# Two combine-and-route stages reordered: sums two batches ahead, logits before ranks, small weights loaded one stage sooner

## The chip, the cores and the metric

The kernel runs on one core of a Trainium2 chip. The metric is the time of one execution on the device in microseconds (us). Three runs of the kernel before gave 2446.49, 2455.0 and 2457.12 us, a median of 2455.0. The profiled execution was a fourth one.

## The reference

Four layers on 4 batches of 512 tokens of 256 float32 numbers (T = 2048 tokens), each layer `x = x + ffn(cond(x))`. What the change touches is the way from one mixture of experts to the next work:

```python
x = x + L0_ffn(L0_cond(x))         # causal attention, ternary linear layer
x = x + L1_ffn(L1_cond(x))         # attention with relative bias; mixture f1: top 2 of 8, capacity, gelu
x = x + L2_ffn(L2_cond(x, cond))   # mixture c2 plus shared expert; mixture f2: top 1 of 8, capacity, relu
x = x + L3_ffn(L3_cond(x))         # attention with relative bias; mixture f3: top 2 of 8, swiglu

# L2_cond
logits = (x @ wt.T + repeat(g @ wg.T, s, axis=0)) / 2
topk_w, topk_idx = top_k(softmax(logits), 2);  topk_w = topk_w / (topk_w.sum(-1) + 1e-20)
y = sum over the two experts of topk_w * ((leaky(x @ w_gate[e]) * (x @ w_up[e])) @ w_down[e])
p = (leaky(x @ sw_gate) * (x @ sw_up)) @ sw_down          # shared expert, every token
y = y + p
# L2_ffn: eidx = argmax(softmax(x @ Wr)); each expert takes its first T/8 tokens (rank = running count)
# L3_cond, bias: h = silu(ln(pos @ w0 + b0, g0)); h = silu(ln(h @ w1 + b1, g1)); h @ w2 + b2
```

## The kernel before

The program is a row of stages. Within a stage every engine has its own instruction list, written out by hand in the order in which it runs, and engines wait for each other on semaphores; between stages all engines meet. Three stages are touched besides two that load weights.

**Stage A** comes after the experts of f1. SP loads the experts' rows (`Combine.sync`, L2027: 8 transfers of 512 KB). DVE adds them to the tokens, batch by batch, with 8 `scalar_tensor_tensor` a batch (`Combine.vector`, L2037: "the sum"). Then tokens are routed to c2. For each batch: PE turns the 4 token tiles (`tensor_turn`, L1491, 8 transposes), ACT copies the turned tokens (L1457), PE makes the logits (`tensor`, L1504 and, for the conditioned router, L1507), DVE takes the best two experts (`vector_ahead`, L1545 to L1570), PE counts ranks (`tensor_after`, L1516 to L1521), DVE makes row numbers (`vector`, L1580 to L1587), and POOL scatters the rows with one indirect DMA for each token tile and choice (`pool`, L1442). After the last batch `vector_last` (L1594 to L1629) makes the list of expert tiles. The same stage runs the shared expert as 18 pipelined steps (16 token tiles): on PE L2082, L2090 and L2098, on ACT L2107 and further, on DVE L2124 and L2129. The weights of the router are loaded by the stage itself, behind the rows:

```python
def sync(self, sp):            # Router, L1401
    sp.dma_start(self.wr_rows[:], self.w_router)...      # 3 loads where the router is conditioned, 1 where not
for b in range(B):             # combine_and_route, PE: turn, logits, two shared steps, ranks, then the next batch
    part.tensor_turn(pe, b)
    part.tensor(pe, b)
    ...
    part.tensor_after(pe, b)
```

The **tile stage** follows: the experts of c2, 40 tiles of tokens, whose rows SP loads one by one (L1865), with four loads of 1 MB of f2's weights between (L1870, `ahead`).

**Stage B** has the same function as stage A, `combine_and_route`, with c2's rows, f2's router and no shared expert, but the relative bias of layer 3 (`RelativeBias`, `rel`): its 8 weights are loaded behind the router's, and its DVE, ACT, POOL and PE steps stand between the batches. `first_hidden` (L230 to L234), `statistics`, `root` on POOL, `normalise` (L254) and `scale` (L260) come after batch 0, the second half after batch 2, `last_product` at the end.

**Stage C** is the input stage of layer 3's attention (`attention_inputs`): DVE first sums f2's rows for all 4 batches (L2037, in `beside`), then takes statistics and normalises, and at last makes the null key and the mask (L435 to L453), for which the product with `inw_wkv` on PE (L651) waits.

Everywhere a copy of the tokens for the second choice (`copy_rows`) is kept for two batches, and the bank of the logits is free again when the ranks of that batch are read (`rank_read`).

Of the kernel before, what the change touches and what calls it, by code (L numbers as in the profile page):

```python
# [20 lines left out]
P = 128  # L21
# [157 lines left out]

class RelativeBias:  # L180
# [5 lines left out]
    def __init__(self, nc, c, l, w, rev, stack, banks):  # L186
        m = Memory(nc, stack, f"rel{l}", side="right")
        self.nc, self.c, self.l, self.w, self.rev = nc, c, l, w, rev
        self.w0, self.b0, self.g0, self.b1, self.g1 = (m.sb(n, [P, D]) for n in ("w0", "b0", "g0", "b1", "g1"))
        self.w1, self.w2, self.b2 = m.sb("w1", [P, KD, D]), m.sb("w2", [P, KD, H]), m.sb("b2", [H, 1])  # L190
# [8 lines left out]
        names = "loaded dist_made hidden link mv_ready rooting rstd_ready scaled pre_ready act_ready t_ready t_copied h_ready o_ready row_ready".split()  # L199
        (self.loaded, self.dist_made, self.hidden, self.link_s, self.mv_ready, self.rooting, self.rstd_ready, self.scaled, self.pre_ready, self.act_ready,  # L200
# [151 lines left out]
def attention_inputs(nc, c, l, iw, stack, block, relative=None):  # L352
# [16 lines left out]
    rel = relative(stack, qt_ps[:].rearrange("p h s -> p (h s)").rearrange("p (k s) -> p k s", k=KD)) if relative is not None else None  # L369
# [8 lines left out]
    if rel is not None:  # L378
        @block.sync
        def _(sp):  # L380
            rel.load(sp)
            rel.store(sp)
# [6 lines left out]
    def _(pool):  # L389
        pool.memset(c.kmask[:], 0.0).then_inc(cleared, 1)  # L390
        for b in range(B):
            pool.wait_ge(mv_ready, QT * (b + 1))
            inverse_root(pool, c, mv[:, b, :, 1], ALU.add, EPS, rooting, b + 1, rstd_ready)
        if cosine:
            pool.wait_ge(null_summed, 1)
            inverse_root(pool, c, nn[:], ALU.max, 1e-24, null_floored, 1, null_root)
# [26 lines left out]
    def _(dve):  # L423
# [928 lines left out]

class Router:
# [1078 lines left out]
```

## Time and profile before

| | |
|---|---|
| median of 3 runs | 2455.0 us |
| the profiled execution, its own time | 2444.63 us |
| its span in the profile | 2442.8 us |
| mean granted TensorE clock | 0.919 of 2.4 GHz |
| PE busy | 2081.4 us (85%) |
| DVE, ACT, POOL busy | 1110.2 (45%), 995.5 (41%), 588.9 us (24%) |
| stage A, from SP's first load to the next stage's | 1202.3 to 1325.3 us |
| tile stage | 1325.3 to 1446.3 us |
| stage B | 1446.3 to 1537.5 us |
| stage C | from 1665.1 us |

Times of rows are microseconds from the span's start. PE is the matmul side of TensorE, SPq the time in which SP's queue writes transfers. A bracket at the end of a row tells how long the engine was idle before it and whose work ended that. A granted clock of 1.00 is 2.4 GHz and one of 0.50 is 1.2 GHz; between them it is the mean of a stretch that had both.

### The profile page before, as it was taken

The numbers are of one execution on the slowest core, as the hardware profiler recorded it, in microseconds if no ns is written. First come the engines' busy times: TensorE is split into PE (matmuls) and PEld (weight loads), VectorE is DVE, ScalarE is ACT, GpSimd is POOL, SyncE is SP. The second block draws the span as 40 slices with busy tenths as digits, with TensorE's granted clock in tenths as the row PEclk, the third lists the DMA queues.
The fourth block names the chain that finished last, engine by engine and source line by source line (L and its number), as shares of the span: only waits on it lengthen the run. The fifth ranks groups of instructions, "written<-read, shape, count | busy, mean of one in ns | idle before, by whom it ended". The sixth has DMA issues, their size and how long they took to land. (4 is left out here: it accounts for less than half of the span.)

```text
span 2442.8 us, 47321 instructions
## 1 busy us (share of the span) xinstructions
PE 2081.4 (85%) x16296; PEld 1466.3 (60%) x16297; DVE 1110.2 (45%) x3373; ACT 995.5 (41%) x2622; POOL 588.9 (24%) x970
## 2 busy tenths in 40 slices
PE   6899999797999994999677854895979999959994
PEld 3477767555777673666455643683557776736663
DVE  5488871455888632010043325115568884321112
ACT  2378871165788611111112321121658774212221
POOL 2121210284111124111131322113831111321111
PEclk9999999898999996999868975897989999969997
DMA  2374402003433113322213240551010003131113
GB/s 79 85 231 133 146 24 90 0 1 104 125 106 106 55 37 103 103 98 90 78 44 110 92 133 26 192 173 40 1 45 21 20 11 129 46 119 44 45 43 111
DMA packets 157136, 197.94 MB, mean 81 GB/s; under 512 B 15315, under 2 KB 130222, under 8 KB 156940
## 3 DMA queue, kind: packets, MB, share of 16 engines
q1 hardware_dynamic: 145228, 169.09, 22.4%
q0 software_dynamic: 11712, 26.26, 3.0%
q8 instruction: 119, 1.95, 0.3%
q14 instruction: 77, 0.63, 0.1%
HBM read 120.60 MB, written 88.90 MB: 86 GB/s over the span
## 5 line engine op out<-in xcount | busy, mean ns | idle before, releaser
L907 ACT ACTIVATE att_pr<-all_h,att_nmax 128x128 f32<-128x128 f32 (+3 forms) x768 | 422.1, 552 | 92.2 <-DVE att_nmax L863 91.0
L965 PEld LDWEIGHTS att_t_ps<-all_ident,att_pr 64*128 64x128 f32 x3840 | 183.6, 139 | 108.2 <-issue 42.9
L965 PE MATMUL att_t_ps<-all_ident,att_pr 64*128 64x64 f32 x3840 | 188.4, 223 | 11.0 <-DVE att_pt L871 10.1
L843 POOL COPY att_rexp<-att_rinv 128x512 f32<-128x512 f32 x96 | 58.6, 610 | 514.8 <-DVE att_rinv L875 514.8
L1133 PE MATMUL out_y_ps<-outw_wo,mem_qt 128*128 128x256 f32 x768 | 178.0, 385 | 0.0
L871 DVE COPY att_pt<-att_t_ps 128x256 f32<-128x256 f32 (+3 forms) x240 | 177.5, 739 | 1.0 <-PE att_t_ps L965 1.0
L1739 PE MATMUL exp_f_h_ps<-exp_f_xs_t,cw_f_w 128*128 128x512 f32 (+1 forms) x512 | 172.2, 495 | 1.5 <-DVE exp_f_xs_t L1776 1.5
L1751 PE MATMUL exp_f_y_ps<-cw_f_w,exp_f_hid 128*128 128x256 f32 x768 | 168.4, 379 | 0.0
L1133 PEld LDWEIGHTS out_y_ps<-outw_wo,mem_qt 128*128 128x128 f32 x768 | 143.5, 191 | 25.0 <-issue 6.8
L1751 PEld LDWEIGHTS exp_f_y_ps<-cw_f_w,exp_f_hid 128*128 128x128 f32 x768 | 144.8, 190 | 19.5 <-issue 0.5
L1806 ACT ACTIVATE exp_f_hid<-exp_f_h_ps 128x512 f32<-128x512 f32 (+1 forms) x128 | 62.4, 490 | 223.3 <-PE exp_f_h_ps L1739 223.1
L863 DVE CUSTOM_DVE_ANT_0 all_h<-att_s_ps,att_bias,mem3k_nsn 128x128 f32<-128x128 f32 (+3 forms) x256 | 130.2, 546 | 46.1 <-PE att_s_ps L953 33.1
L863 DVE CUSTOM_DVE_ANT_0 all_h<-att_s_ps,att_bias,mem1k_nsn 128x128 f32<-128x128 f32 (+3 forms) x256 | 130.2, 546 | 45.9 <-PE att_s_ps L953 33.9
L863 DVE CUSTOM_DVE_ANT_0 all_h<-att_s_ps,att_bias,mem0k_nsn 128x128 f32<-128x128 f32 (+3 forms) x256 | 130.2, 547 | 42.8 <-POOL att_bias L826 24.8
L907 ACT ACTIVATION_READ_ACCUMULATOR att_pr<-all_h,att_nmax 128x1 f32 x768 | 144.9, 189 | 0.0
L1739 PEld LDWEIGHTS exp_f_h_ps<-exp_f_xs_t,cw_f_w 128*128 128x128 f32 x512 | 99.4, 195 | 68.6 <-issue 61.0
L919 ACT ACTIVATE att_pt<-att_t_ps 128x1024 f32<-128x1024 f32 (+1 forms) x144 | 116.7, 810 | 31.5 <-PE att_t_ps L965 31.5
L669 PE MATMUL in_q_ps<-inw_wq,all_xt 128*128 128x512 f32 x256 | 120.3, 615 | 2.8 <-ACT all_xt L566 2.8
L1718 POOL DMA_INDIRECT expert_f<-exp_f_ys,exp_f_idx x48 | 46.7, 972 | 305.6 <-DVE exp_f_ys L1785 254.5
L1982 DVE COPY til_f_xs_t<-til_f_x_ps 128x256 f32<-128x256 f32 x40 | 17.0, 425 | 195.6 <-PE til_f_x_ps L1904 195.6
L988 PE MATMUL att_o_ps<-att_pt,mem0k_v 128*64 128x128 f32 x1280 | 97.7, 282 | 1.5 <-DVE mem_qt L882 0.4
L988 PE MATMUL att_o_ps<-att_pt,mem1k_v 128*64 128x128 f32 x1280 | 97.7, 282 | 1.5 <-DVE mem_qt L882 0.4
(395 smaller groups left out, 3900.5 us busy)
## 6 DMA issues: line engine op xcount, KB each, us to landing
sorted_c<-all_zero SPq DMA_DIRECT2D x8, 2056.0 KB, 13.8
sorted_f<-all_zero SPq DMA_DIRECT2D x8, 2056.0 KB, 11.9
cw_f_w<-in_L_ffn_w_dram SPq DMA_DIRECT2D x16, 1024.0 KB, 8.0
cw_f_w<-in_L_ffn_W_dram SPq DMA_DIRECT2D x16, 1024.0 KB, 8.0
com_f_rows<-expert_f SPq DMA_DIRECT2D x20, 512.0 KB, 6.7
band<-rev SPq DMA_DIRECT2D x2, 4096.0 KB, 19.4
att_bias<-band SPq DMA_DIRECT2D x32, 256.0 KB, 3.2
til_c_xs<-sorted_c SPq DMA_DIRECT2D x40, 128.5 KB, 2.1
```

Source lines behind the costliest of these rows:

```text
L669: last = nc.tensor.matmul(q_ps[t % 2][:, n, :], c.xt[:, k, P * t:P * (t + 1)], wq[:, k, S * n:S * (n + 1)], start=(k == 0), stop=(k == KD ...
L843: pool.tensor_copy(rexp[:], group_ap(rinv, G).unsqueeze(3).to_broadcast([P, B, 2, DH])).then_inc(rexp_ready, 1)
L863: nc.vector.tensor_tensor_reduce(sc[p % 4][:, hh, 0:n], s_ps[(2 * p + hh) % 3][:, 0:n], bias_ap(i, q, hh), -1.0, c.nsn[:, b, q, h:h + 1], ...
L871: nc.vector.tensor_copy(*pt_and_turned(p)).then_inc(t_copied[e % 2], 1)
L907: nc.scalar.activation(pr[p % 4][:, hh, 0:n], sc[p % 4][:, hh, 0:n], ACT.Exp, scale=-1.0, bias=nmax[:, b, q, h:h + 1], accum_out=rsum[:, b ...
L919: nc.scalar.activation(*pt_and_turned(p), ACT.Copy).then_inc(t_copied[e % 2], 1)
L965: last = nc.tensor.transpose(t_ps[e % 2][:, n, (q + 1) * hh + kb, :], pr[p % 4][d, hh, P * kb:P * (kb + 1)], c.ident[d, d])
L988: last = nc.tensor.matmul(o_ps[DH * hh:DH * (hh + 1), p % B, :], c.v[:, QT * b + kb, :], pt[p % 4][:, P * ((q + 1) * hh + kb):P * ((q + 1) ...
L1133: nc.tensor.matmul(y_ps[b % 2][:, q, :], c.out_t[:, p, S * b + P * q:S * b + P * (q + 1)], wo[:, p, :], start=(p == 0), stop=False)
L1739: last = nc.tensor.matmul(h_ps[f % 4][:, 0:cap], w1_sb[n][:, k, P * f:P * (f + 1)], xs_t[n][:, k, :], start=(k == 0), stop=(k == KD - 1))
L1751: last = nc.tensor.matmul(y_ps[(YT * n + t // 2) % 2][:, t % 2, :], hid[n][:, f, P * t:P * (t + 1)], w2_sb[n][:, f, :], start=(f == 0), st ...
L1806: nc.scalar.activation(hid[n][:, f, :], h_ps[f % 4][:, 0:cap], func).then_inc(hid_ready, 1)
```

## The change

The small weights move into the stage before (`RouterWeights`, `RelativeWeights`): three loads for stage A go ahead of the other `ahead` loads of f1's experts, nine loads for stage B go ahead of the four 1 MB loads of the tile stage. `combine_and_route` is replaced by one function for each stage. Both sum two batches ahead; the logits of batch b+1 stand before the ranks of batch b, which a semaphore of its own (`logits_read`) allows; the copies for the second choice are kept for all 4 batches; in stage A `vector_last` stands after shared step 10 instead of last; in stage B the bias's first half stands ahead of the sums. The condition's part of the logits is one matmul for a batch, ahead of the others, where it was one for each token tile. Stage C makes the null key and mask first and takes sums, statistics and normalisation in turn.

```diff
-        for t in range(QT):
-            for k in range(KD):
-                last = self.nc.tensor.matmul(self.l_ps[:, t, :], self.xt_of(b)[:, k, P * t:P * (t + 1)], self.wr[:, k, :], start=(k == 0),
-                                             stop=(k == KD - 1 and self.cond is None))
-            if self.cond is not None:
-                last = self.nc.tensor.matmul(self.l_ps[:, t, :], self.g_t[:, b:b + 1].to_broadcast([DH, P]), self.wg_t[:], start=False, stop=True)
+            pe.wait_ge(self.logits_read, b)
+            if self.one_bank:
+                pe.wait_ge(self.rank_read, b)
+        if rw.conditioned:
+            self.nc.tensor.matmul(self.l_ps[:, 0:QT, :], rw.g_t[:, b:b + 1].to_broadcast([DH, P]), rw.wg_t[:].unsqueeze(1).to_broadcast([DH, QT, E]),
+                                  start=True, stop=False)
...
-            copy_rows = m.sb("copy_rows", [P, 2 * QT, W])[:] if mx.top == 2 else None
+            copy_rows = m.sb("copy_rows", [P, NT, W])[:] if mx.top == 2 else None
...
+def combine_and_share(nc, c, com, part, shx, block):   # stage A, DVE:
+        com.vector(dve, 0)
+        com.vector(dve, 1)
+        part.vector_ahead(dve, 0)
+        com.vector(dve, 2)
+        shx.vector(dve, 0)
+        part.vector(dve, 0)
+        part.vector_ahead(dve, 1)
+        shx.vector(dve, 1)
+        com.vector(dve, 3)
...
+        for t in range(7, NT + 2):
+            shx.vector(dve, t)
+            if t == 10:
+                part.vector_last(dve)
...
+        part.tensor_after(pe, 0)
+        shx.tensor(pe, 1)
+        part.tensor_turn(pe, 2)
+        part.tensor(pe, 2)
+        shx.tensor(pe, 2)
+        part.tensor_after(pe, 1)
...
+def combine_and_relate(nc, c, com, part, rel, block):  # stage B, DVE:
+        rel.first_hidden(dve)
+        rel.statistics(dve, 0)
+        rel.normalise(dve, 0)
+        rel.scale(dve, 0)
         com.vector(dve, 0)
...
+        com.vector(dve, 1)
+        part.vector_ahead(dve, 0)
+        com.vector(dve, 2)
+        part.vector(dve, 0)
+        rel.copy_turned(dve, 0)
+        part.vector_ahead(dve, 1)
+        com.vector(dve, 3)
+        part.vector(dve, 1)
+        rel.second_hidden(dve)
+        rel.statistics(dve, 1)
+        part.vector_ahead(dve, 2)
+        part.vector(dve, 2)
+        rel.normalise(dve, 1)
+        rel.scale(dve, 1)
+        part.vector_ahead(dve, 3)
+        part.vector(dve, 3)
+        rel.copy_turned(dve, 1)
         part.vector_last(dve)
+        rel.last_row(dve)
...
-            experts_by_tile(nc, c, c2, tw, sorted_rows["c2"], done["c2"], r_c2, ahead=cw.loads)
+            experts_by_tile(nc, c, c2, tw, sorted_rows["c2"], done["c2"], r_c2, ahead=rw.loads + relw.loads + cw.loads)
...
+        if com is not None:                             # stage C, DVE:
+            null_and_mask()
+            com.vector(dve, 0)
+            statistics(0)
+            com.vector(dve, 1)
+            normalise(0)
```

On PE, at the start of stage A, these rows stood behind batch 0's logits: two shared steps (`shx`), the ranks (`turn_c_r_ps`) and then batch 1's turn and logits.

```order
L2082 MATMUL shx_gu_ps<-shw_wgu,all_xt 128x512 x4
L2090 MATMUL shx_t_ps<-all_ident,shx_hid 128x128 x2
L1516 MATMUL turn_c_r_ps<-route_c_sel,all_before 128x32
L1521 MATMUL turn_c_r_ps<-route_c_sel,all_ones_b 128x24
L1521 MATMUL turn_c_r_ps<-route_c_sel,all_ones_b 128x16
L1521 MATMUL turn_c_r_ps<-route_c_sel,all_ones_b 128x8
L1491 MATMUL turn_c_x_ps<-all_ident,all_x 128x128 x8
```

After the change PE's rows from the start of stage A are these, with turn and logits of batches 0 and 1 ahead of the first shared step.

```order
L1531 MATMUL turn_c_x_ps<-all_ident,all_x 128x128 x8
L1546 MATMUL turn_c_l_ps<-rw_c_wg_t,rw_c_g_t 128x32
L1550 MATMUL turn_c_l_ps<-rw_c_wr,all_xt 128x8 x8
L1531 MATMUL turn_c_x_ps<-all_ident,all_x 128x128 x8
L1546 MATMUL turn_c_l_ps<-rw_c_wg_t,rw_c_g_t 128x32
L1550 MATMUL turn_c_l_ps<-rw_c_wr,all_xt 128x8 x8
L2129 MATMUL shx_gu_ps<-shw_wgu,all_xt 128x512 x2
L1562 MATMUL turn_c_r_ps<-route_c_sel,all_before 128x32
```

Batch 1's turn and logits moved ahead of batch 0's ranks, and of the two shared steps one now stands between logits and ranks.

In stage B, PE had turn, logits and ranks of batch 0, then the turn of batch 1.

```order
L1491 MATMUL turn_f_x_ps<-all_ident,all_h 128x128 x8
L1504 MATMUL turn_f_l_ps<-route_f_wr,all_xt 128x8 x8
L1516 MATMUL turn_f_r_ps<-route_f_sel,all_before 128x32
L1521 MATMUL turn_f_r_ps<-route_f_sel,all_ones_b 128x24
L1521 MATMUL turn_f_r_ps<-route_f_sel,all_ones_b 128x16
L1521 MATMUL turn_f_r_ps<-route_f_sel,all_ones_b 128x8
L1491 MATMUL turn_f_x_ps<-all_ident,all_h 128x128 x8
```

Now the bias's first turn (`relps_banks<-all_ident,rel_act`), the turn and the logits of batch 1 stand between batch 0's logits and its ranks, and the bias's product (L297) behind batch 2's logits.

```order
L1531 MATMUL turn_f_x_ps<-all_ident,all_h 128x128 x8
L1550 MATMUL turn_f_l_ps<-rw_f_wr,all_xt 128x8 x8
L290 MATMUL relps_banks<-all_ident,rel_act 128x128 x8
L1531 MATMUL turn_f_x_ps<-all_ident,all_h 128x128 x8
L1550 MATMUL turn_f_l_ps<-rw_f_wr,all_xt 128x8 x8
L1562 MATMUL turn_f_r_ps<-route_f_sel,all_before 128x32
L1567 MATMUL turn_f_r_ps<-route_f_sel,all_ones_b 128x24
L1567 MATMUL turn_f_r_ps<-route_f_sel,all_ones_b 128x16
L1567 MATMUL turn_f_r_ps<-route_f_sel,all_ones_b 128x8
L1531 MATMUL turn_f_x_ps<-all_ident,all_h 128x128 x8
L1550 MATMUL turn_f_l_ps<-rw_f_wr,all_xt 128x8 x8
L297 MATMUL relps_banks<-relw_w,rel_act_t 128x256 x8
```

PE thus meets the ranks of a batch one batch later than before, with the next batch's logits done.

SP's queue in the tile stage, behind the first tile loads, was the last four rows of this list alone; what stands ahead of them is new.

```order
L1917 DMA rw_f_wr<-in_L_ffn_Wr_dram 128x2x8
L1917 DMA relw_w<-in_L_cond_w_dram 128x256
L1917 DMA relw_b<-in_L_cond_b_dram 128x256
L1917 DMA relw_g<-in_L_cond_g_dram 128x256
L1917 DMA relw_b<-in_L_cond_b_dram 128x256
L1917 DMA relw_g<-in_L_cond_g_dram 128x256
L1917 DMA relw_w<-in_L_cond_w_dram 128x2x256
L1917 DMA relw_w<-in_L_cond_w_dram 128x2x16
L1917 DMA relw_b<-in_L_cond_b_dram 16x1
L1917 DMA cw_f_w_0<-in_L_ffn_W_dram 128x2x1024
L1917 DMA cw_f_w_0<-in_L_ffn_W_dram 128x8x256
L1917 DMA cw_f_w_1<-in_L_ffn_W_dram 128x2x1024
```

The loads of the later tiles stand behind these thirteen, where they stood behind four.

## Rows read from the trace of the kernel before

**Rows 1.** Windows: stretch, length, busy us of PE, PEld, DVE, ACT, POOL; clock; DMA, GB/s.

```profile
1217.00:1257.00 40.00, 30.24 (x105) 21.93 (x105) 16.14 (x63) 7.56 (x18) 9.29 (x9) 0.63 0.07 27
1257.00:1290.00 33.00, 27.25 (x94) 20.27 (x95) 12.59 (x51) 6.33 (x14) 14.98 (x15) 0.60 0.18 65
1290.00:1321.00 31.00, 29.28 (x113) 17.85 (x111) 12.74 (x37) 13.22 (x35) 8.07 (x8) 0.99 0.10 35
...
1345.00:1440.00 95.00, 81.36 (x476) 59.07 (x474) 35.62 (x148) 31.31 (x113) 37.07 (x38) 0.98 0.29 90
1446.00:1500.00 54.00, 18.12 (x86) 15.99 (x87) 23.07 (x78) 5.59 (x8) 10.06 (x16) 0.50 0.36 115
```

**Rows 2.** Timeline of stage A's start: start, length, engine, line, operation, wait.

```profile
1207.59 3.38 DVE L2037 SCALAR_TENSOR_TENSOR all_x<-com_f_rows,r_f_weight,all_x 128x256 f32<-128x256 f32 x8 [12.70 <-DMA com_f_rows<-expert_f]
...
1217.30 0.38 PE L1481 MATMUL turn_c_r_ps<-all_ident,route_c_wr_rows 8*128 8x8 f32 x2 [23.14 <-DMA route_c_wg_t<-in_L_cond_wg_dram]
...
1219.62 1.09 ACT L1457 ACTIVATE all_xt<-turn_c_x_ps 128x512 f32<-128x512 f32 x2 [1.72 <-PE turn_c_x_ps L1491]
...
1226.76 0.19 DVE L1545 COPY route_c_lg<-turn_c_l_ps 128x32 f32<-128x32 f32 x1 [15.79 <-PE turn_c_l_ps L1507]
...
1237.60 1.73 PE L1491 MATMUL turn_c_x_ps<-all_ident,all_x 128*128 128x128 f32 x7 [4.10 <-DVE all_x L2037]
```

**Rows 3.** Timeline of stage A's tail.

```profile
1299.85 1.88 PE L2082 MATMUL shx_gu_ps<-shw_wgu,all_xt 128*128 128x512 f32 x4
...
1302.65 1.88 PE L2082 MATMUL shx_gu_ps<-shw_wgu,all_xt 128*128 128x512 f32 x4
...
1316.99 0.16 DVE L1594 COPY route_c_count<-turn_c_r_ps 128x8 f32<-128x8 f32 x1
...
1323.61 0.19 DVE L1626 TENSOR_TENSOR r_c_weight<-r_c_weight,route_c_total 128x32 f32<-128x32 f32 x1
...
1325.30 3.67 SPq L1865 DMA_DIRECT2D til_c_xs<-sorted_c  x4
```

**Rows 4.** Groups of POOL in stage A: count, busy us, mean ns, idle before.

```profile
L1442 POOL DMA_INDIRECT sorted_c<-all_x,r_c_pos x16 | 16.4, 1028 | 65.1 <-DVE r_c_pos L1587 61.4 <-issue 3.7
```

**Rows 5.** Timeline of SP's queue early in the tile stage.

```profile
1329.01 2.40 SPq L1870 DMA_DIRECT2D cw_f_w<-in_L_ffn_W_dram  x4
1335.91 0.36 SPq L1865 DMA_DIRECT2D til_c_xs<-sorted_c  x1
```

**Rows 6.** Timeline of SP's queue in stage B, small weights.

```profile
1453.45 1.42 SPq L1406 DMA_DIRECT2D route_f_wr<-in_L_ffn_Wr_dram  x1
...
1458.58 0.67 SPq L215 DMA_DIRECT2D rel_b<-in_L_cond_b_dram  x1
```

**Rows 7.** Timeline of stage B.

```profile
1451.67 1.67 DVE L2037 SCALAR_TENSOR_TENSOR all_h<-com_c_rows,r_c_weight,all_h 128x256 f32<-128x256 f32 x4 [15.39 <-DMA com_c_rows<-expert_c]
...
1461.08 1.21 PE L1504 MATMUL turn_f_l_ps<-route_f_wr,all_xt 128*128 128x8 f32 x5 [5.19 <-DMA route_f_wr<-in_L_ffn_Wr_dram]
...
1464.67 0.19 DVE L1545 COPY route_f_lg<-turn_f_l_ps 128x32 f32<-128x32 f32 x1 [9.62 <-PE turn_f_l_ps L1504]
...
1467.86 0.16 DVE L230 CAST rel_dist<-rel_dist_i 128x4 f32<-128x4 int32 x1
...
1475.13 1.38 DVE L254 TENSOR_SCALAR rel_hid<-rel_hid,rel_mv 128x256 f32<-128x256 f32 x4 [3.54 <-POOL rel_mv L106]
...
1502.69 5.07 PE L290 MATMUL relps_banks<-rel_w,rel_act_t 128*128 128x256 f32 x16
...
1517.25 1.09 PE L1491 MATMUL turn_f_x_ps<-all_ident,all_h 128*128 128x128 f32 x4 [9.49 <-DVE all_h L2037]
...
1532.06 0.97 POOL L1442 DMA_INDIRECT sorted_f<-all_h,r_f_pos  x1 [0.30 <-issue]
...
1537.49 0.91 SPq L1675 DMA_DIRECT2D exp_f_xs<-sorted_f  x2
```

**Rows 8.** Timeline of stage C.

```profile
1693.70 1.57 PE L651 MATMUL in_x_ps<-inw_wkv,all_xt 128*128 128x144 f32 x5 [3.22 <-DVE inw_wkv L453]
```

More of the change, by code:

```diff
@@ L376, in attention_inputs, with _ @@
     wide_q = [(b, i) for b in range(B) for i in range(HP)]
[L378 to L381, printed above, removed]
+    @block.sync
+    def _(sp):
+        if com is not None:
+            com.sync(sp)
+        for to, weight, semaphore in rel_loads:
+            sp.dma_start(to, weight).then_inc(semaphore, 16)
+        if rel is not None:
             rel.store(sp)
@@ L457, in statistics @@
                 dve.wait_ge(c.x_loaded[b], 16)
+            if com is not None:
+                dve.wait_ge(com.added, QT * (b + 1))
             for t in range(QT):
@@ L2148, in _ @@
         part.pool_first(pool)
-        if rel is not None:
-            rel.distances(pool)
         for b in range(B):
             part.pool(pool, b)
-            if rel is not None and b % 2 == 0:
-                rel.root(pool, b // 2)
         part.pool_last(pool)
@@ L2159, in _ @@
         part.scalar_first(a)
+        part.scalar(a, 0)
+        part.scalar(a, 1)
+        part.scalar_double(a, 0)
+        shx.scalar(a, 0)
+        shx.scalar(a, 1)
+        part.scalar(a, 2)
+        part.scalar_double(a, 1)
+        shx.scalar(a, 2)
+        shx.scalar(a, 3)
+        part.scalar(a, 3)
+        part.scalar_double(a, 2)
+        shx.scalar(a, 4)
+        shx.scalar(a, 5)
+        part.scalar_double(a, 3)
+        shx.scalar(a, 6)
+        part.scalar_last(a)
+        for t in range(7, NT + 2):
+            shx.scalar(a, t)
@@ new lines, in _ @@
+    @block.tensor
+    def _(pe):
+        part.tensor_second(pe)
+        part.tensor_turn(pe, 0)
+        part.tensor(pe, 0)
+        part.tensor_turn(pe, 1)
+        part.tensor(pe, 1)
+        shx.tensor(pe, 0)
+        part.tensor_after(pe, 0)
[4 more added lines that the diff above has]
+        part.tensor_after(pe, 1)
+        shx.tensor(pe, 3)
+        part.tensor_turn(pe, 3)
+        part.tensor(pe, 3)
+        shx.tensor(pe, 4)
+        part.tensor_after(pe, 2)
+        shx.tensor(pe, 5)
+        shx.tensor(pe, 6)
+        part.tensor_after(pe, 3)
+        for t in range(7, NT + 2):
+            shx.tensor(pe, t)
@@ new lines, in combine_and_relate, with _ @@
+def combine_and_relate(nc, c, com, part, rel, block):
+    @block.sync
+    def _(sp):
+        com.sync(sp)
+        part.sync(sp)
+        rel.store(sp)
+    @block.gpsimd
+    def _(pool):
+        rel.distances(pool)
+        part.pool_first(pool)
+        rel.root(pool, 0)
+        part.pool(pool, 0)
+        part.pool(pool, 1)
+        rel.root(pool, 1)
+        part.pool(pool, 2)
+        part.pool(pool, 3)
+        part.pool_last(pool)
+    @block.scalar
+    def _(a):
+        part.scalar_first(a)
+        rel.activate(a, 0)
```

260 lines of the change are left out of this document (129 added, 131 removed).

## The prediction

> **What bounds the kernel now.** I read the page's busy shares first: PE is busy 85% of the span, so what the change can win lies where PE is not. The windows show where that is [rows 1]: in stage A PE is busy 30.24 of 40 us and 27.25 of 33 us, but at a granted clock of 0.63 and 0.60, and only behind that, where the shared steps run without the routing, 29.28 of 31 us at 0.99. In stage B it is busy 18.12 of the first 54 us, at 0.50. The tile stage is PE's own: 81.36 of 95 us at 0.98. Then I read the timelines, for the wait that ends last in each stage. In stage A the sums are ready at 1207.59 plus some, yet PE starts at 1217.30, released by the load of `wg_t` [rows 2]; later it waits 4.10 us for batch 1's sum (1237.60), since DVE comes to that sum only after routing batch 0. In stage B it waits 5.19 us for `wr` and 9.49 us for the last batch's sum [rows 7]. Both stages end with a serial tail: in A `vector_last`, 1316.99 to 1323.80, then the next stage's first load at 1325.30 [rows 3]; in B the last scatter, 1532.06, and the next stage 5.43 us later, 4.45 after the scatter's end.
>
> **The change, stage A.** I walk through the new order with the durations of the rows.
> - Start. The three small loads are gone from this stage, so PE turns batch 0 as soon as its sum is there. Eight sums take 3.38 us [rows 2], the last tile's turn can start at about 1211, and turn 0 ends at 1211.6. ACT's copy takes 1.09 us: 1212.8. Twelve logits matmuls took from 1220.7 to 1226.76, 0.50 us each [rows 2]; nine, one of them wider, take about 4.2 at this clock: 1216.9. Turn 1 (1.9) and its copy: 1220.0; logits 1: 1224.2. Before, batch 0's logits were there at 1226.76.
> - Clock. With PE dense from 1212 on I take the full clock from 1225. In the first 40 us of before it was full for a quarter of the time (0.63), with the waits of 3 to 4 us in between.
> - Steady part. A shared step takes 2.80 us at the full clock (1299.85 to 1302.65) [rows 3]. From 1224.2: 16 steps 44.8; turns 2 and 3, 2.1; logits 2 and 3, 4.2; the two waits for ACT's copy of the turn, 2.4; the ranks 1.0; 1.0 more for what still runs at the low clock; the pipeline's end 1.9. That is 57.4, or 1281.6. DVE's share in a step is 0.87 us, so its other work (for a batch: `vector_ahead` 3.5, the row numbers 0.9, the sums 3.4, against two steps' free time of 3.9 and more where a turn and logits stand between) fits in.
> - `vector_last`. Behind step 10 DVE is away for 6.8 us [rows 3]; PE has two `gu` buffers and some 4.3 us of work in hand, and the step itself has 0.9 of DVE, so PE waits 6.8 + 0.9 − 4.3 = 3.4 us: 1285.0. In before it stood behind all steps, where it cost 3.6 us after ACT's last copy.
> - After that wait the clock. Waits of 3 to 4 us stand all through the stretches at 0.63 and 0.60 [rows 1, 2]; so I let it fall, for the 6 steps behind it at most, and take 6 us: 1291. The Trainium skill, page "TensorE: Matmul & The Clock Gate", section "Loop structure matters more than you think", says the same of a loop with a wait between bursts of matmuls, that PE then runs cold. By it the 6 us stand and stage A gives 33; were only the gap paid, it would give 39.
> - POOL: 32 scatters of 1.03 us [rows 4] and 0.30 of issue are 42 us from about 1230 on, to 1272, so they hide behind the shared steps.
> - The next stage's first load comes 1.5 us behind the end [rows 3]: 1292.5 against 1325.3, **−33** (−25 if the low clock lasts longer, −39 if it doesn't fall at `vector_last`). The three loads that move to f1's experts cost SP three issues of about 1 us where it waits for the experts: 0, at most 1.
>
> **The tile stage.** The nine small loads took SP 1453.45 to 1459.25, 5.8 us, in stage B [rows 6]. Here they stand ahead of four 1 MB loads and of the loads for the later tiles, and the rows of those come behind. SP had 1331.41 to 1335.91 idle [rows 5], about 3.4 of it free after the loop's own start. So 2.4 us are lost at the least, 5.8 at most and a little for the transfers: **+5**. The cover would be tiles loaded further ahead; there are only the first four.
>
> **Stage B.** The stage begins at SP's first load, 1446.3 on the old clock; rows arrive at 1451.67 [rows 7].
> - The bias's first half needs no rows. It took DVE 9.9 us from 1467.86 on, 3.54 of them a wait for POOL's root [rows 7], which had scatters ahead of it; without these I take 1.5 for the wait and 7.7 for the whole: 1447.2 to 1454.9. It ends 3.2 us after the rows came, and sums 0 and 1 go to 1458.3 and 1461.7. So batch 0 is later than in before, by 3.
> - Turn 0 ends 1458.8; its logits need no load now: 1460.0 to 1463.6 (before 1461.08 to 1464.67). Bias turn and turn 1 to 1467.5, logits 1 1472.3, rank 0 1472.5; turn 2 1474.5, logits 2 1479.3; the bias's product (5.07 [rows 7]) 1484.4; turn 3 1486.6; logits 3 wait for `logits_read` of batch 2 and end 1492.9. PE has no wait of 9 us for a sum: the waits for `all_h` of before disappear but for the first.
> - Then DVE: batch 2's slots, `normalise` and `scale` 1497.1, `vector_ahead` 3 1499.0, rank 1499.3, slots 1500.6. Four scatters of 0.97 + 0.30: 1501.5 to 1506.6. The next stage starts 4.45 later: 1511.0 against 1537.5, **−27** (everything at the low clock, as in before at 0.50; −31 if it rises for the second half, −23 if DVE's steps, of which there are seven between batch 2's logits and the last scatter, each end 0.5 later).
> - The last bias product (3.6) lies beside the scatters.
>
> **Stage C.** The null work (1684.93 to 1693.6, in front of the kv product at 1693.70 [rows 8]) goes to the start, where DVE waited for f2's rows. With sums and statistics in turn normalise(0) comes about 1.5 us later, but the 3.22 us wait for `inw_wkv` is gone: **−2** (0 to −3).
>
> **Sum.** −33 + 5 − 27 − 2 = −57 us. The profiled execution of before took 2444.63 us, so the changed one would take 2388 by its own clock. The median of the runs of before is 2455.0, 10 above the profiled one; against it the forecast is 2398. Less than about 12 us either way (0.5%) can't be told from no change for this kernel.
>
> **Rivals.**
> 1. *More clock.* No fall behind `vector_last` (+6) and a clock that rises in stage B, where PE has fewer gaps (+5): −68, 2387. Against it: stage B's 54 us at 0.50 [rows 1]. 0.15.
> 2. *The low clock lasts in A.* The ranks wait for `vector_ahead` in every batch; if that holds the clock at 0.5 until 1250, 25 us at a step of about 5.2 instead of 2.8 lose about 12: 2410. The stretch to 1257 at 0.63 speaks for it, the missing 3 to 4 us waits against it. 0.12.
> 3. *The order gives back its gain.* Queues run in order, so a DVE that sums ahead delays `vector_ahead`, and PE waits for ranks instead of sums; only the loads (about 13 us less wait in A and B) and the merged matmuls are left: about −13, 2442. Against it: the walk through DVE has slack of 1 to 2 us for each batch. 0.05.
> 4. *Slower: TensorE stays at 1.2 GHz through stage A and the tile stage.* It needs PE to be broken up so often that the clock doesn't rise: A's 16 steps at 5.2 instead of 2.8 us and the rest cost 40, the tile stage with 81.36 us busy at 0.98 [rows 1] about 65 more; −57 + 105 = +48, 2503. It ends slower than before once the low clock holds for more than some 29 us of the tile stage. What speaks against it is that stage A of before, with more waits, came to 0.99 by 1290. 0.03.
> 5. Rest: a wait that I don't see, of up to 30 us. Such a one takes −57 to −27, so faster still. 0.05.
>
> **How the numbers follow.** The forecast has 0.60: 2398. Bounds of its terms: A −25 to −39, tile +2.4 to +6, B −23 to −31, C 0 to −3, f1 0 to 1: from −42 to −70 at the ends; the ends don't all meet, so 2383 to 2414. With rivals 1 and 2, and a part of 5, the range is 2380 to 2420. Faster by more than 12 us: forecast, 1, 2, 5 and half of 3, 0.92; within: 0.05; slower: 0.03.
>
> **What would show it.** In the changed profile PE's first row of stage A at about 1210 without `wg_t` in its bracket; the clock in the 40 us behind above 0.8; `vector_last` between shared steps and one wait of 3 us on PE there; SP's first tile load at 1292 ± 5; the tile stage 121 + 5 us long; in stage B no PE wait for `all_h` over 4 us but the first, and 65 us from SP's first load to the next stage's (91 before); in stage C no wait for `inw_wkv`. Wrong would be: stage A's waits for ranks in place of those for sums, or a tile stage over 130 us.

## The result and the profile after

The changed kernel takes 2392.81 us (median of 4 runs, 2390.49 to 2396.12) against 2450.74 us (4 runs, 2446.44 to 2457.12) beside it: 57.9 us less, a ratio of 0.9761 (95% interval 0.9744 to 0.9779). The forecast was 57 less, 2398 us against a median of 2455.0, with a range of 2380 to 2420.

The spans of the two profiles are 2442.8 and 2390.2 us, 52.6 apart. I cut both at the same points of SP's queue (the first row load of stage A, of the tile stage, of stage B, of f2's experts, of stage C, and the first bias load of layer 3's attention). The table does the same for each experiment below.

| us | before | after | forecast | moved |
|---|---|---|---|---|
| up to stage A | 1202.3 | 1205.6 | 0 to +1 | +3.3 |
| stage A | 123.0 | 92.8 | −33 | −30.3 |
| tile stage | 121.0 | 127.7 | +5 | +6.6 |
| stage B | 91.2 | 61.2 | −27 | −30.0 |
| f2's experts | 127.6 | 128.6 | 0 | +1.0 |
| stage C to the attention | 126.0 | 122.4 | −2 | −3.6 |
| the rest | 651.7 | 652.0 | 0 | +0.3 |

The 3.3 us ahead of stage A are not the moved loads: f1's experts, whose queue got them, take 243.1 us against 243.9, and the time is lost in the 958 us before them. There the change moves code between classes and gives f1's router one more semaphore, and the length differs by up to 6 us among the profiles of the kernels below (959.6 to 965.9 us). All of these are longer than the 958.4 us of before, of which there is one profile; that a part of the difference is the change's isn't excluded. The profile of before is one of the fastest runs of its kernel, which is why the medians are further apart than the profiles.

The windows of the trace after (columns as in [rows 1]) answer to those of before. In the routing part PE is busy for nine tenths (13.82 of 15 and 21.65 of 24 us), where it was busy for 76% and 83% at a clock of 0.63 and 0.60.

```profile
1217.00:1232.00 15.00, 13.82 (x52) 10.74 (x53) 7.14 (x27) 2.51 (x5) 0.00 (x0) 0.51 0.16 51
1232.00:1256.00 24.00, 21.65 (x95) 14.59 (x94) 14.55 (x60) 7.87 (x18) 16.02 (x16) 0.79 0.25 88
1256.00:1283.00 27.00, 23.16 (x92) 13.62 (x91) 17.09 (x61) 11.14 (x28) 15.65 (x16) 1.00 0.23 79
1283.00:1287.00 4.00, 4.00 (x10) 1.83 (x9) 0.00 (x0) 0.68 (x3) 0.00 (x0) 0.58 0.00 0
1287.00:1296.00 9.00, 8.13 (x32) 5.01 (x31) 2.54 (x6) 3.60 (x11) 0.00 (x0) 1.00 0.00 0
1426.00:1447.00 21.00, 9.06 (x40) 8.03 (x40) 16.00 (x49) 3.49 (x5) 2.19 (x8) 0.50 0.63 200
1447.00:1470.00 23.00, 17.01 (x94) 15.23 (x94) 15.25 (x59) 3.19 (x6) 8.80 (x10) 0.72 0.13 46
```

The timeline of PE in stage A of the kernel after, with the next stage's first load as its last row, answers to [rows 2, 3]:

```profile
1213.12 1.97 PE L1531 MATMUL turn_c_x_ps<-all_ident,all_x 128*128 128x128 f32 x8 [7.13 <-DVE all_x L2084]
1216.27 0.63 PE L1546 MATMUL turn_c_l_ps<-rw_c_wg_t,rw_c_g_t 64*128 64x32 f32 x2 [1.18 <-ACT all_xt L1496]
...
1227.39 3.76 PE L2129 MATMUL shx_gu_ps<-shw_wgu,all_xt 128*128 128x512 f32 x4
...
1242.50 1.96 PE L2129 MATMUL shx_gu_ps<-shw_wgu,all_xt 128*128 128x512 f32 x4
...
1250.55 3.76 PE L2129 MATMUL shx_gu_ps<-shw_wgu,all_xt 128*128 128x512 f32 x4
...
1281.95 0.44 PE L2137 MATMUL shx_t_ps<-all_ident,shx_hid 128*128 128x128 f32 x2 [3.78 <-DVE shx_hid L2176]
...
1298.36 3.67 SPq L1912 DMA_DIRECT2D til_c_xs<-sorted_c  x4
```

The waits for a sum are gone but the first; the load of `wg_t` is in no bracket. The same shared matmul takes 3.76 us at 1227.4, 1.96 at 1242.5 and 3.76 again at 1250.6: the clock rose at 1232 and fell again for some microseconds. Over the 40 us from the first turn on it is hardly higher than the 0.63 of before:

```profile
1213.10:1253.10 40.00, 35.28 (x146) 25.55 (x147) 24.71 (x93) 10.70 (x23) 14.69 (x15) 0.67 0.30 100
```

In the tile stage (PE, then SP's queue) the fifth tile's rows come late by more than before, where it was 5.17 us:

```profile
1323.91 0.69 PE L1951 MATMUL til_c_x_ps<-all_ident,til_c_xs 128*128 128x128 f32 x2 [11.75 <-DMA til_c_xs<-sorted_c]
...
1306.46 4.56 SPq L1917 DMA_DIRECT2D cw_f_w<-in_L_ffn_W_dram  x4
1312.18 17.43 SPq L1912 DMA_DIRECT2D til_c_xs<-sorted_c  x4
```

In stage B (PE) the one long wait is that for the rows and the bias's first half; two of 3.6 and 5.5 us remain at the end, both for DVE, and no load is waited for [rows 7].

```profile
1436.67 1.97 PE L1531 MATMUL turn_f_x_ps<-all_ident,all_h 128*128 128x128 f32 x8 [18.56 <-DVE all_h L2084]
...
1466.71 3.03 PE L1550 MATMUL turn_f_l_ps<-rw_f_wr,all_xt 128*128 128x8 f32 x16 [3.61 <-DVE route_f_lg L1591]
...
1475.38 0.21 PE L1562 MATMUL turn_f_r_ps<-route_f_sel,all_before 128*128 128x32 bf16 x1 [5.52 <-DVE route_f_sel L1608]
...
1487.16 0.91 SPq L1722 DMA_DIRECT2D exp_f_xs<-sorted_f  x2
```

### The profile page after: what moved, and what is told of

The parts are those of the page before. It is cut to its first block and busy times, and to the rows that moved or that the text cites. A ratio compares the mean times of both kernels' runs of the same rounds, so it can differ in the third digit from the quotient of the medians.

```text
span 2390.2 us, 47281 instructions
## 1 busy us (share of the span) xinstructions
PE 2071.5 (87%) x16272; PEld 1454.0 (61%) x16273; DVE 1118.4 (47%) x3373; ACT 995.8 (42%) x2622; POOL 589.3 (25%) x970
## 5 line engine op out<-in xcount | busy, mean ns | idle before, releaser
L894 DVE CUSTOM_DVE_ANT_0 all_h<-att_s_ps,att_bias,mem1k_nsn 128x128 f32<-128x128 f32 (+3 forms) x256 | 130.2, 546 | 45.7 <-PE att_s_ps L984 34.1
L1019 PE MATMUL att_o_ps<-att_pt,mem3k_v 128*64 128x128 f32 x1280 | 97.7, 282 | 1.5 <-DVE mem_qt L913 0.6
```

The costliest lines, as they stand in the source:

```text
L894: nc.vector.tensor_tensor_reduce(sc[p % 4][:, hh, 0:n], s_ps[(2 * p + hh) % 3][:, 0:n], bias_ap(i, q, hh), -1.0, c.nsn[:, b, q, h:h + 1], ...
L1019: last = nc.tensor.matmul(o_ps[DH * hh:DH * (hh + 1), p % B, :], c.v[:, QT * b + kb, :], pt[p % 4][:, P * ((q + 1) * hh + kb):P * ((q + 1) ...
```

## The experiments

Each starts from the changed kernel. Times are medians of 4 runs (5 for the last) with the ratio to the kernel before beside it and its interval; what an edit did is read from the stage lengths of its profile, since a stage whose code isn't touched repeats: stage A within 0.3 us (the last four kernels apart), the tile stage within 1.0 (but 120.2 and 122.6 us where the loads are spread, with the same code). Stage B comes in two lengths, 61.0 to 61.3 and 63.0 us, whatever was edited, and the granted clock goes with them: from 21 to 44 us into the stage it is 0.70 to 0.72 in the five short ones (0.72 in the changed kernel's row above) and 0.65 in the six long ones, as in the run with `vector_last` at the end:

```profile
1447.00:1470.00 23.00, 17.99 (x87) 16.24 (x87) 14.34 (x56) 2.35 (x5) 7.72 (x8) 0.65 0.12 41
```

PE's two long waits for DVE are the same in both, 3.61 and 5.52 us. What decides between the two clocks is open, and a difference of 2 us in stage B is not put down to an edit here.

| us | stage A | tile | B | C | median | ratio |
|---|---|---|---|---|---|---|
| after | 92.8 | 127.7 | 61.2 | 122.4 | 2392.8 | 0.976 (0.974 to 0.978) |
| A in the old order | 108.2 | 127.3 | 63.0 | 121.7 | 2410.3 | 0.983 (0.980 to 0.986) |
| B in the old order | 92.9 | 126.9 | 87.5 | 122.1 | 2421.1 | 0.987 (0.985 to 0.989) |
| loads in their own stages | 100.4 | 120.9 | 77.9 | 122.4 | 2411.2 | 0.983 (0.980 to 0.986) |
| `vector_last` at the end | 90.6 | 127.6 | 63.0 | 121.6 | 2393.3 | 0.975 (0.973 to 0.977) |
| small loads behind the tile loop | 92.9 | 121.6 | 61.0 | 122.3 | 2389.1 | 0.973 (0.971 to 0.975) |
| big loads spread as well | 93.1 | 120.2 | 61.1 | 121.8 | 2386.0 | 0.972 (0.970 to 0.974) |
| condition as four matmuls | 100.4 | 127.8 | 63.0 | 121.7 | 2399.9 | 0.978 (0.975 to 0.981) |
| C in the old order | 92.7 | 127.9 | 61.2 | 126.1 | 2398.6 | 0.977 (0.975 to 0.979) |
| shared step in the ACT gap; all loads behind | 110.6 | 119.3 | 63.0 | 122.3 | 2400.5 | 0.978 (0.974 to 0.981) |
| `vector_last` in pieces; small loads behind | 96.9 | 121.3 | 61.3 | 121.6 | 2395.1 | 0.976 (0.974 to 0.978) |
| idle matmuls at A's start; all loads behind | 100.7 | 118.6 | 63.0 | 122.3 | 2392.2 | 0.974 (0.971 to 0.976) |
| `vector_last` at the end; loads spread | 101.6 | 122.6 | 63.0 | 122.2 | 2402.0 | 0.978 (0.976 to 0.980) |

**Stage A in the old order.**

```diff
 # combine_and_share, PE (DVE and ACT likewise in the order of before)
-        part.tensor_turn(pe, 0); part.tensor(pe, 0); part.tensor_turn(pe, 1); part.tensor(pe, 1); shx.tensor(pe, 0); part.tensor_after(pe, 0) ...
+        for b in range(B):
+            part.tensor_turn(pe, b); part.tensor(pe, b); shx.tensor(pe, 2 * b); shx.tensor(pe, 2 * b + 1); part.tensor_after(pe, b)
```

> The changed kernel with stage A's queues in the order of before; loads, merged matmul, four-batch copies and stages B and C stay changed. Stage A took 123.0 us before and 92.8 after. Theory (the order carries it): the loads and the merged matmul alone give 8 to 12 us of the 30, so stage A takes 111 to 115 us and the kernel 2411 to 2415; PE waits again 3 to 4 us before the turns of batches 1 to 3 and the clock stays near 0.6 in the routing part. Rival (the loads carry it): stage A takes 98 us or less and the kernel under 2399.

Stage A takes 108.2 us. PE's rows show the three waits of before again, to a tenth:

```profile
1228.50 1.79 PE L1531 MATMUL turn_c_x_ps<-all_ident,all_x 128*128 128x128 f32 x8 [4.09 <-DVE all_x L2084]
...
1246.76 1.94 PE L1531 MATMUL turn_c_x_ps<-all_ident,all_x 128*128 128x128 f32 x8 [3.20 <-DVE all_x L2084]
...
1264.52 1.94 PE L1531 MATMUL turn_c_x_ps<-all_ident,all_x 128*128 128x128 f32 x8 [3.21 <-DVE all_x L2084]
```

So the order is worth 15.5 us here, 10.5 of them these waits; loads and the merged matmul are worth 14.8, more than the 8 to 12 that I gave them. Neither of the two theories has it all: the gain is in halves. The old order has `vector_last` at the end, which is worth 2.1 us by itself (below), so against the new order with `vector_last` at the end (90.6 us) the order of the batches is worth 17.6.

**Stage B in the old order.** The edit is the same kind in `combine_and_relate`, on PE, DVE, ACT and POOL.

> The changed kernel with stage B's queues in the order of before; everything else stays changed. Stage B took 91.2 us before and 61.2 after. Theory: the loads' wait is worth 5 us, the order 25: stage B takes about 86 us and the kernel about 2417. Rival (the bias's first half ran late mainly because its weights were late): stage B takes under 75 us and the kernel under 2407.

Stage B takes 87.5 us, so the order is worth 26.3 of the 30.0 us and the loads 3.7. The waits for the sums, 13.41, 3.57 and 9.49 us on PE, stand where they stood (13.39, 3.58 and 9.49 us), though no load is waited for.

```profile
1457.75 1.94 PE L1531 MATMUL turn_f_x_ps<-all_ident,all_h 128*128 128x128 f32 x8 [13.41 <-DVE all_h L2084]
...
1471.85 1.94 PE L1531 MATMUL turn_f_x_ps<-all_ident,all_h 128*128 128x128 f32 x8 [3.57 <-DVE all_h L2084]
...
1495.30 1.94 PE L1531 MATMUL turn_f_x_ps<-all_ident,all_h 128*128 128x128 f32 x8 [9.49 <-DVE all_h L2084]
```

**The loads in their own stages, in the new order.**

```diff
-            experts_by_capacity(..., ahead=rw.loads + sw.loads + tw.loads + [tw.load_d])
+            experts_by_capacity(..., ahead=sw.loads + tw.loads + [tw.load_d])
-            experts_by_tile(..., ahead=rw.loads + relw.loads + cw.loads)
+            experts_by_tile(..., ahead=cw.loads)
 # and rw.loads (A, B) and relw.loads (B) behind com.sync in the stage itself
```

> The changed kernel with the small weights loaded where the kernel before loads them (behind the rows, in stages A and B), in the new order. Theory: stage A starts its logits 7 us later (PE waits for the last small load) and takes 98 to 100 us; stage B, where the bias now stands ahead of the sums, is held by the nine loads and takes 70 to 75 us, 9 to 14 more; the tile stage falls from 127.7 to about 121. Sum +9 to +15: 2402 to 2408. Rival (the loads were the gain, the order cost nothing alone): 2420 or more.

Stage A is 7.6 us longer, as expected, and the tile stage 6.7 shorter. Stage B is 16.8 longer, more than the 9 to 14 expected, and the kernel's 2411.2 us lie above the 2402 to 2408. PE's first row of A and DVE's bias row of B name the loads:

```profile
1222.29 0.38 PE L1521 MATMUL turn_c_r_ps<-all_ident,rw_c_wr_rows 8*128 8x8 f32 x2 [23.17 <-DMA rw_c_wg_t<-in_L_cond_wg_dram]
...
1446.07 1.67 DVE L241 SCALAR_TENSOR_TENSOR rel_hid<-relw_w,rel_dist,relw_b 128x256 f32<-128x256 f32 x4 [16.52 <-DMA relw_b<-in_L_cond_b_dram]
```

The early loads are worth 3.7 us to B's old order and 16.8 to its new one, which has the bias at the head of DVE's queue: in stage B the two halves of the change need each other. In stage A they don't: there the loads are worth 7.6 us to the new order and some 7 to the old one (14.8 less the condition's 7.6, below, if that holds in the old order as well). With them the sum of A closes too: 92.8 + 15.5 (order) + 7.6 (loads) + 7.6 (condition, below) = 123.5, against 123.0 measured.

**`vector_last` at the end of stage A.**

```diff
         for t in range(7, NT + 2):
             shx.vector(dve, t)
-            if t == 10:
-                part.vector_last(dve)
+        part.vector_last(dve)
```

> The changed kernel with the list of expert tiles (vector_last) at the end of stage A again instead of behind shared step 10. The wait of PE for it was 3.8 us after the change. Forecast's theory (the gap costs itself and 6 us of clock): stage A is 3.8 + 6 shorter on PE and 4 longer in the tail, so 87 us. Rival (the clock dips for 3 us only): 3.8 + 1.5 gained, 4 to 7 lost in the tail: 92 to 95 us, the kernel 2391 to 2395.

Stage A takes 90.6 us, 2.1 less, which lies in neither expectation (87, and 92 to 95). From the ranks of batch 3 to PE's end it is 28.9 us (34.6 after), and from there to the next stage 5.1 (1.7 after). So behind step 10 it costs PE 5.7 us: the wait of 3.78 and 1.9 of clock, not the 3.4 + 6 of the forecast; the tail it saves is 3.5 us. Its place behind step 10 is a loss of 2 us, small enough that the kernel's median doesn't show it.

**The small loads behind the tile loop.**

```diff
-            experts_by_tile(..., ahead=rw.loads + relw.loads + cw.loads)
+            experts_by_tile(..., ahead=cw.loads, behind=rw.loads + relw.loads)
```

> The changed kernel with the nine small loads of the tile stage behind the loop of tile loads instead of ahead of the four 1 MB loads. Theory: they cost the tile stage the 6.6 us by which PE's wait for the fifth tile grew (5.17 to 11.75 us); the stage falls from 127.6 to 121 us and stage B, where the weights then land at about the time of the rows, stays at 61 to 63. Kernel 2386 to 2388. Rival (they only move): stage B grows by what the tile stage loses, kernel 2392.

The tile stage falls to 121.6 us and B doesn't grow. In the groups of waits, PE's wait for tile rows is 5.3 at its longest again:

```profile
PE til_c_x_ps L1953 <- DMA til_c_xs<-sorted_c: 9.1, 2, 5.3
```

**The 1 MB loads spread over the first four rounds as well.**

```diff
+            for at, loads in enumerate(between):          # one 1 MB load each, four rounds unrolled
+                for n in range(G):
+                    sp.wait_ge(xt_ready, at * G + n + 1)
+                    sp.wait_ge(idx_copied, at * G + n + 1)
+                    load(at * G + G + n, n)
+                for dst, src, semaphore in loads:
+                    sp.dma_start(dst, src).then_inc(semaphore, 16)
-            with sp.Fori(0, R - 1) as i:
+            with sp.Fori(len(between), R - 1) as i:
```

> As the run with the small loads behind the loop, and the four 1 MB loads one behind each of the first four rounds of tile loads instead of all ahead of the first round. Theory: PE's wait for the fifth tile is the time in which 4 MB land ahead of it, and vanishes: tile stage 112 to 117 us, kernel 2377 to 2383. Rival (4 MB have to pass in any case and each holds up the tile loads behind it): 119 us or more.

The wait of 5.3 us is gone, and yet the stage is only 1.4 us shorter: the rival was right. In its place PE waits four times for tile rows that stand behind a big load, 0.28, 1.15, 0.23 and 1.23 us, 2.9 together:

```profile
1335.14 0.44 PE L1960 MATMUL til_c_x_ps<-all_ident,til_c_xs 128*128 128x128 f32 x2 [1.15 <-DMA til_c_xs<-sorted_c]
...
1358.12 0.44 PE L1960 MATMUL til_c_x_ps<-all_ident,til_c_xs 128*128 128x128 f32 x2 [1.23 <-DMA til_c_xs<-sorted_c]
```

These two waits are most of what the windows show, where PE is busy 7.18 and 7.66 of 10 us while a big load passes, against 8.63 where none does; behind the wait of 1.23 us the clock falls to 0.85 for one window.

```profile
1330.00:1340.00 10.00, 7.18 (x43) 4.96 (x42) 3.58 (x16) 2.67 (x11) 3.50 (x4) 1.00 0.60 186
...
1350.00:1360.00 10.00, 7.66 (x42) 5.20 (x42) 3.73 (x16) 2.59 (x11) 3.18 (x4) 0.98 0.63 197
1360.00:1370.00 10.00, 9.08 (x50) 7.35 (x51) 3.15 (x13) 3.26 (x12) 3.36 (x4) 0.85 0.27 80
...
1380.00:1390.00 10.00, 8.63 (x53) 6.29 (x53) 3.84 (x17) 3.31 (x12) 3.87 (x5) 1.00 0.33 104
```

This is the fastest kernel of the study, 2386.0 us (2385.41 to 2386.63); its interval lies just below that of the changed kernel. How much of that is the spreading isn't shown: the last kernel below has the same tile stage, and it took 122.6 us there, more than the 121.6 without spreading.

**The condition as four matmuls a batch,** as in the kernel before.

> The changed kernel with the condition's part of the logits as four 128x8 matmuls a batch, as before, instead of one 128x32. Theory: three more short matmuls a batch at 0.45 us (low clock) or 0.25 us (full) each stand on PE's path: stage A 96 to 98 us instead of 92.8. Rival: it is hidden, 93 us.

Stage A takes 100.4 us, 7.6 more and past my range. PE's rows of batches 0 and 1 stand 9.0 us apart, where they stood 7.1 apart (1216.27 to 1223.39): 1.9 us a batch at the low clock.

```profile
1216.79 1.02 PE L1547 MATMUL turn_c_l_ps<-rw_c_wr,all_xt 128*128 128x8 f32 x4 [1.18 <-ACT all_xt L1496]
1225.83 1.02 PE L1547 MATMUL turn_c_l_ps<-rw_c_wr,all_xt 128*128 128x8 f32 x4 [1.18 <-ACT all_xt L1496]
```

Batches 2 and 3 cost as much. From the first row of their logits to the shared step behind them it is 4.01 and 4.83 us, against 2.15 and 2.96 after the change, since the clock falls sooner: inside batch 2's logits, as their last group shows (0.61 us for the groups ahead of it), and earlier within batch 3's.

```profile
1242.28 0.99 PE L1547 MATMUL turn_c_l_ps<-rw_c_wr,all_xt 128*128 128x8 f32 x4
...
1243.72 3.78 PE L2128 MATMUL shx_gu_ps<-shw_wgu,all_xt 128*128 128x512 f32 x4
```

Four times 1.9 are the 7.6 us; what the shared steps between gain and lose (−0.3, +1.0 and −0.8) cancels.

**Stage C in the old order.**

> The changed kernel with stage C's order of before. Theory: stage C with the projections behind it, from SP's first load to the attention's first, took 126.0 us before and 122.4 after; it goes back to 125.5 to 126.5, kernel 2395 to 2397. Rival (the 3.6 us are chance): 122 to 123.

126.1 us: the 3.6 to 3.7 us are the order's. PE starts 15.2 us behind SP's first load, where it starts 17.1 behind it after the change, but then waits for `inw_wkv`. The two rows account for 2.5 of the 3.7 us (4.4 less 1.9); the rest wasn't traced.

```profile
1644.31 3.78 PE L671 MATMUL in_x_ps<-inw_wkv,all_xt 128*128 128x144 f32 x16 [4.44 <-DVE inw_wkv L467]
```

**Four kernels whose stage A was disturbed.** The last four try to improve on the changed kernel. The first has a shared step ahead of the logits of batches 2 and 3 (`turn, shx, logits` for `turn, logits, shx`) and all thirteen loads of the tile stage behind the loop:

> Two edits in stages that don't overlap. Stage A: the shared step stands between the turn and the logits of batches 2 and 3, where PE waited 1.18 us for ACT's copy. Theory: the two waits go (2.4 us), and if they were what let the clock dip behind them (0.60 and 0.50 to 0.56 in the trace after the change) the dips go too: stage A 87 to 90 us against 92.8; rival (the dips come from elsewhere): 90 to 92. Tile stage: all thirteen loads behind the loop. Theory: the wait of 5.3 us that the four 1 MB loads still caused goes, 115 to 117 us, and the 4 MB are landed before stage B's rows; rival: they hold up the last stores or the rows, tile stage and stage B together 182 us or more.

The second cuts `vector_last` into five pieces behind shared steps 9 to 13 (a generator with four yields):

> Stage A: vector_last in five pieces behind shared steps 9 to 13, each smaller than DVE's 1.92 us of free time in a step. Theory: neither PE's wait of 3.8 us with its dip of the clock nor the tail: 87 to 88.5 us against 92.8 (behind step 10) and 90.6 (at the end). Rival (PE is held elsewhere): 90 or more. Tile stage as in the run with the small loads behind the loop: 121 to 122 us.

The third runs matmuls without use at the stage's start:

```diff
         part.tensor_second(pe)
+        shx.warm(pe, 4)        # wait for the shared weights, then 4 x matmul(gu_ps[1], ident, wgu[:, 0])
         part.tensor_turn(pe, 0)
```

> Stage A: four matmuls of 128x512 without use run on PE while it waits for the rows (7.1 us), into a bank that no one reads yet. Theory (the clock rises by PE being busy without a break): turn and logits of batches 0 and 1, 17 us of PE at 1.2 GHz, run at 2.4 GHz in part; stage A 86 to 90 us. Rival (the waits of 1.18 us behind each turn keep it low, or let it fall again): 92 to 93, or more where the four matmuls end behind the sum. Tile stage as in the run with all loads behind the loop.

The last has `vector_last` at the end and the spread loads, each of which had been measured:

> The two edits that shortened a stage in a trace of their own, together: vector_last at the end of stage A (90.6 us) and the loads of the tile stage spread over its first rounds with the small ones behind the loop (120.2 us). Theory (the stages add): stage A 90.6, tile stage 120.2, stage B 61 to 63, kernel 2382 to 2386, and none of the late semaphores that the traces of the three kernels run together before this one show in stage A. Rival (such late semaphores come with the order after the change and can hit any run): stage A 95 us or more again.

All four have a stage A of 97 to 111 us. In their traces, and in none of the other ten, ACT and PE stand still together for some microseconds in the middle of the shared steps. ACT's releaser is given as "remote" or "issue", so nothing of the kernel that the profile shows; PE's is "issue" or ACT. ACT's rows of the second and of the last of them:

```profile
1266.54 0.38 ACT L2170 ACTIVATE shx_hid_t<-shx_t_ps 128x256 f32<-128x256 f32 x1 [2.45 <-issue]
1272.15 0.38 ACT L2173 ACTIVATE all_h<-shx_y_ps 128x256 f32<-128x256 f32 x1 [5.22 <-remote]
```

```profile
1261.50 0.38 ACT L2168 ACTIVATE shx_hid_t<-shx_t_ps 128x256 f32<-128x256 f32 x1 [3.16 <-remote]
1269.26 0.38 ACT L2171 ACTIVATE all_h<-shx_y_ps 128x256 f32<-128x256 f32 x1 [7.38 <-remote]
```

In two of the four the edit isn't the cause: in the second kernel the standstill lies ahead of the first piece of `vector_last`, and stage A of the last is, instruction for instruction, the one that took 90.6 us. For the first and the third it was not separated. These four ran on two other chips than the eight before them, and on these two chips the kernel before took its usual 2455.3 and 2454.6 us. No single kernel of the new order was run on both pairs of chips, so whether the chip is the cause, and why the old order should be spared, stays open. The last expectation's theory fell (stage A 101.6 and not 90.6, tile stage 122.6 and not 120.2, kernel 2402.0 and not 2382 to 2386), and its rival holds only so far as these two chips go. The four medians therefore say little of the edits. Rows ahead of the first standstill, or behind the last, still do:
- Pieces: from the ranks of batch 3 to PE's end 31.2 us, 1.9 of them one matmul at the low clock left by the standstill, so 29.3 and a tail of 1.7. That is 31.0 against 36.3 (behind step 10) and 34.1 (at the end). Read from the rows, not from a time of the whole.
- The idle matmuls raise the clock ahead of turn 0, but it falls again during batch 0's logits, and the first shared step starts 20.3 instead of 21.8 us into the stage. The logits of batches 0 and 1:

```profile
1207.00 6.33 PE L2153 MATMUL shx_gu_ps<-shw_wgu,all_ident 128*128 128x512 f32 x8
1214.55 1.63 PE L1531 MATMUL turn_c_x_ps<-all_ident,all_x 128*128 128x128 f32 x8 [1.22 <-DVE all_x L2086]
...
1217.69 2.27 PE L1550 MATMUL turn_c_l_ps<-rw_c_wr,all_xt 128*128 128x8 f32 x16
...
1223.49 3.58 PE L1550 MATMUL turn_c_l_ps<-rw_c_wr,all_xt 128*128 128x8 f32 x16
```

- The shared step in ACT's gap trades the 1.18 us for a wait for DVE:

```profile
1235.15 0.44 PE L2139 MATMUL shx_t_ps<-all_ident,shx_hid 128*128 128x128 f32 x2 [1.52 <-DVE shx_hid L2178]
```

- All loads behind the loop: the tile stage takes 119.3 and 118.6 us, not the 115 to 117 expected; with stage B 182.2 and 181.6, against 181.3 with the loads spread. Stage B has its long length in both and its short one in the last, so by the tile stage alone they are 0.9 and 1.6 us ahead of 120.2, less than the 2.4 by which the spread loads' own tile stage differed between two kernels. No gain is shown.

## Why the prediction was right, and where it wasn't

- **Stage A, start.** Forecast: the first shared step 21.9 us into the stage. Measured: 21.8. The loads' part (7.6 us) came out as PE's wait for `wg_t` had it. What the merged matmul is worth was not a term of its own; the walk implied about 5 us, the run showed 7.6.
- **Stage A, clock.** This term was mis-sized, in both directions. I took the full clock 23 us into the stage; it came at 26 us and fell twice more, at 1238 and 1250, each time with no more than the 1.18 us wait for ACT's copy, short logits matmuls and bf16 ranks ahead of it. The sign that asked for a clock above 0.8 in these 40 us did not come (0.67 against 0.63 before); what came is that the stretch at a mean clock of 0.6 to 0.7 ends at 1256, where it ended at 1290. From the first shared step on, without `vector_last`, PE took 63.6 us where the sum had 57.4. Against that `vector_last` cost 5.7 us, not 9.4. The Trainium skill, page "TensorE: Matmul & The Clock Gate", section "Loop structure matters more than you think", has PE run cold where each burst of matmuls stands behind a long wait. The trace agrees in kind (0.58 from 1283 to 1287, behind the wait of 3.78) and gives the price of the fall, 1.9 us, a third of what I took. The two errors, 6.2 us too few and 3.7 too many, cancel to 2.7 with the tail's 0.2.
- **Stage A, `vector_last`.** The forecast charged its place but never compared it with the old one by rows. The runs did: 2.1 us lost against the end.
- **POOL hidden.** Right: its last scatter starts at 1277.2, 21 us before the next stage.
- **Tile stage.** Right in mechanism, but the term was too small: +5 forecast with bounds of +2.4 and +6, +6.6 measured, all of it in one wait (5.17 to 11.75). The 3.4 us of SP's slack, my lower bound, did not help, since the wait is for the landing of what is queued and not for SP.
- **Stage B.** Forecast −27 (the walk gives −26.5), with everything at the low clock; measured −30.0. Turn 0 ended 12.6 us into the stage, forecast 12.5. Then the clock rose in parts (0.72 from 1447 to 1470), which is half of the rival "more clock": the bias's product ended 36.0 us into the stage, not 38.1. At least 1.9 us of the miss go with the clock: at 0.65 instead of 0.72 stage B takes 63.0 us. Behind the first there is no PE wait for `all_h` over 4 us, as forecast; the wait of 5.5 us is for batch 3's choice, and the walk has it too (logits end 1492.9, `vector_ahead` 1499.0).
- **Stage C.** Forecast −2 with a bound of −3, measured −3.6; the wait that went is 4.4 us in the changed kernel with C's old order, and not 3.2.
- **f1's experts.** 0, as forecast.
- **Rivals.** That the order gives its gain back fell with the two old-order runs (15.5 and 26.3 us). The second, a low clock that lasts in A, came in part: the steady part lost 6.2 us, where that rival had 12, and 1.9 us of price at `vector_last` where the forecast had 6 hid it. The slower rival needed a low clock through the tile stage, whose windows show 0.95 from 1318 to 1420.

The total was better than its parts: the terms missed by +2.7, +1.6, −3.0 and −1.6. That they add up to −57.3 against −57 is luck; with stage B at its other length of 63.0 us it would be −55.4. Two of the sums on record are slightly off as well: the bounds of the terms end at −41 and −71, not −42 and −70, and the chances of a gain over 12 us add up to 0.945, not 0.92. The forecast rests on neither.

## What to carry to other kernels

Read a stage that is bound by waits between engines as a queue problem: walk each engine's new order with durations of rows, and the result can be had to some 3 us in 60 to 90. An early load is worth what the order makes of it: stage B's loads were worth 3.7 us to the old order and 16.8 to the new one, which needs them first, while stage A's were worth 7 to 8 to both. And loads that move to a stage that is "full" cost there what they delay, measured at the first consumer that waits; put them behind the last transfer that this stage needs (6.0 us here).

## What the runs showed of the hardware

- The granted clock fell from 2.4 to 1.2 GHz for 3 to 7 us behind waits of no more than 1.18 us among short matmuls, and behind a wait of 3.78 us between long ones; matmuls without use, run for 6.3 us ahead of the work, raised it, and it fell again during the first logits.
- While a 1 MB load passes, the tile rows queued behind it come late: PE waited 0.2 to 1.2 us for them four times, and was busy 7.2 to 8.0 us in ten instead of 8.6.
- Four 128x8 matmuls with an operand of their own in place of one 128x32 cost 1.9 us a batch, at the low clock all along (batches 0 and 1) or where it falls within the logits (2 and 3).
- In four traces, on two chips, ACT and PE stood still together for 2 to 7 us several times in stage A, with no releaser of the program's; the other ten traces, eight of them on two other chips, have none. Where the code was the same it cost 11 us of stage A (101.6 against 90.6). Not explained.
